# An attention and feed-forward layer whose split activation h is stored with its two parts interleaved

## What is computed

```
x = fwht(x * SU_ug) / 64
x_up   = x @ W_up.T   * (Wscale_ug[:2048] * 64)
x_gate = x @ W_gate.T * (Wscale_ug[2048:] * 64)
h = silu(x_gate) * x_up                      # 4096 tokens x 2048
x = fwht(h * SU_dp) / 64
x = x @ W_down.T * (Wscale_dp * 64)          # back to 512 columns
```

## Time and profile before

| | us |
|---|---|
| median of 3 runs | 1592.2 |
| lowest and highest run | 1590.52 and 1594.0 |
| the profiled execution's own time | 1590.71 |
| its span, from the first to the last instruction | 1588.9 |

### The profile page before, as it was taken

The page is one execution under the profiler, slowest core; times in us unless marked ns, Lnnn a source line. Parts: engine busy times, 40 slices in busy tenths (PEclk is TensorE's granted clock), DMA queues, the critical chain, the costliest instruction groups (busy, mean ns, idle before and its releaser), DMA issues.

```text
span 1588.9 us, 26579 instructions
## 1 busy us (share of the span) xinstructions
PE 1537.9 (97%) x10280; PEld 1385.6 (87%) x10280; DVE 1040.3 (65%) x1771; ACT 616.2 (39%) x1257; POOL 465.6 (29%) x584
## 2 busy tenths in 40 slices
PE   6999999999998799999999999999999999999997
PEld 5987988888887688889999999999999999999996
DVE  6766776677676699875575475566466557557544
ACT  4153244235225555433433343343343333333322
POOL 5365456447337533500030030030040021013001
PEclk9999999999999999999999999999999999999999
DMA  7031122122222497587668677857776867766861
GB/s 270 1 120 60 34 87 93 34 81 100 70 77 84 185 374 275 212 293 278 236 218 297 220 253 246 279 204 257 268 245 220 307 203 258 276 242 212 281 229 63
DMA packets 92060, 307.44 MB, mean 193 GB/s; under 512 B 9888, under 2 KB 10272, under 8 KB 90144
## 3 DMA queue, kind: packets, MB, share of 16 engines
q1 hardware_dynamic: 90928, 301.54, 53.8%
q10 hardware_dynamic: 1008, 4.20, 0.7%
HBM read 255.37 MB, written 50.33 MB: 192 GB/s over the span
## 4 chain that ended last, share of the span: by engine, by line
PE 61%; DVE 5%; ACT 1%; DMA 1%; issue 1%; SPq 0%; POOL 0%; ACTq 0%; POOLq 0%; DVEq 0%
PE ff_bank_b L1840 16%; PE ff_bank_c L1840 10%; PE ff_bank_a L1840 10%; PE ff_acc L105 7%; PE ff_acc L107 7%; PE ff_acc L106 7%; DVE ff_d_lo L1639 2%; DMA gu_scratch<-ff_ring 1%; DVE ff_ring L1629 1%; PE ff_x_ps L1791 1%; ACT at_union L578 1%; PE ff_x_ps L1811 1%; PE ff_x_ps L1799 0%; DVE ff_c L1685 0%; PE ff_x_ps L1800 0%
## 5 line engine op out<-in xcount | busy, mean ns | idle before, releaser
L1840 PE MATMUL ff_bank_b<-ff_x_hi,ff_ring 128*128 128x256 f32 x1536 | 303.5, 280 | 4.5 <-DVE ff_c L1685 4.2
L1840 PEld LDWEIGHTS ff_bank_b<-ff_x_hi,ff_ring 128*128 128x128 f32 x1536 | 248.6, 188 | 6.3 <-issue 4.5
L1840 PE MATMUL ff_bank_b<-ff_x_lo,ff_ring 128*128 128x256 f32 x768 | 214.7, 280 | 0.0
L105 PE MATMUL ff_acc<-ff_d_hi,ff_h_hi 128*128 128x512 f32 x512 | 203.9, 398 | 2.7 <-DVE ff_d_lo L1639 2.7
L1840 PE MATMUL ff_bank_c<-ff_x_hi,ff_ring 128*128 128x256 f32 x1024 | 205.8, 284 | 0.0
L1840 PE MATMUL ff_bank_a<-ff_x_hi,ff_ring 128*128 128x256 f32 x1024 | 203.5, 282 | 0.0
L107 PE MATMUL ff_acc<-ff_d_hi,ff_h_lo 128*128 128x512 f32 x512 | 199.8, 390 | 0.0
L106 PE MATMUL ff_acc<-ff_d_lo,ff_h_hi 128*128 128x512 f32 x512 | 199.4, 389 | 0.0
L1840 PEld LDWEIGHTS ff_bank_c<-ff_x_hi,ff_ring 128*128 128x128 f32 x1024 | 166.2, 189 | 2.2 <-issue 2.0
L1840 PEld LDWEIGHTS ff_bank_a<-ff_x_hi,ff_ring 128*128 128x128 f32 x1024 | 165.3, 188 | 2.7 <-DVE ff_ring L1629 0.2
L1679 DVE TENSOR_TENSOR ff_c<-ff_bank_b,ff_c 128x512 f32<-128x512 f32 x64 | 44.2, 690 | 163.8 <-PE ff_bank_b L1840 163.8
(11 more groups left out here) (306 smaller groups left out, 3523.7 us busy)
## 6 DMA issues: line engine op xcount, KB each, us to landing
ff_ring<-gu_scratch SPq DMA_DIRECT2D x392, 512.0 KB, 4.9
gu_scratch<-ff_ring SPq DMA_DIRECT2D x56, 512.0 KB, 7.6
at_xt<-in_xt SPq DMA_DIRECT2D x4, 2048.0 KB, 8.4
at_xn<-in_x SPq DMA_DIRECT2D x32, 256.0 KB, 3.0
x_scratch<-at_x SPq DMA_DIRECT2D x32, 256.0 KB, 2.0
ff_raw<-in_wgu SPq DMA_DIRECT2D x8, 1024.0 KB, 7.7
at_wd_a<-in_wd SPq DMA_DIRECT2D x8, 512.0 KB, 4.1
mixed_scratch<-at_wd_a SPq DMA_DIRECT2D x8, 512.0 KB, 3.5
```

Source lines behind the costliest of these rows:

```text
L105: pe.matmul(out, lhs_hi, rhs_hi, start=first, stop=False)
L1840: i = pe.matmul(bank[:, m, :], r[:, a, m, c, :], b[:, k, c, :], start=(k < 3 and m == 0 and c == 0 and b is x_hi and a == 0), stop=(m == 1 ...
```

## The change

The two parts of h get one tile per buffer, with an innermost axis of two; the high part is element 0 of that axis, the low part element 1. Everything that reads or writes `h_hi` and `h_lo` keeps its code and now goes through these views.

```diff
-        h_hi = [sb(f"h_hi{i}", [P, 2, FB], F32R) for i in range(2)]
-        h_lo = [sb(f"h_lo{i}", [P, 2, FB], F32R) for i in range(2)]
+        h = [sb(f"h{i}", [P, 2, FB, 2], F32R) for i in range(2)]
+        h_hi, h_lo = [h[i][:, :, :, 0] for i in range(2)], [h[i][:, :, :, 1] for i in range(2)]
```

## The result

Seven runs of each kernel: before 1592.2 us (1590.52 to 1594.49), after 1598.95 us (1597.36 to 1602.27); the ratio is 1.005 [1.004, 1.0059]. The change costs 6.75 us, 0.4%. That lies in the range of the prediction, but the forecast case, no effect that can be told, is refuted.

A forecast was written before the change was run, and what follows sets the result against it. The prediction took TensorE to bound the kernel. Its terms for weight loads, the matmul beside them, and ScalarE and VectorE were all 0, leaving the median at 1592 us; range 1588 to 1609 us.

The forecast's parts named there:

- the forecast case: Whole kernel: no effect that can be told, 1589 to 1595.4 us; chance 58%.
- What bounds the kernel: TensorE, busy for 97% of the span; one nanosecond more per down matmul is 1.5 us.
- Weight load, taken at 112 ns: The 1536 down weight loads: stepped load as long as a contiguous one, hidden under 227 ns matmuls, 0 us.
- The upper bound of 224 ns: Down weight loads: twice the contiguous time, still hidden inside a down, 4.5 us at 42 entries behind 256-column matmuls.
- doubled loads: Down entries: loads of twice the length make the first down matmul 106 ns late, 4.5 us in all; chance 7%.
- the cliff: Down matmuls: loads of 336 ns pass 227 ns and set the pace, costing 167 us; chance 6%.
- ScalarE and VectorE: Rounding and subtraction of h: stepped access adds at most 0.41 us per instruction, taken as 0 because of slack.
- The first block: VectorE, 88% busy there: sixteen longer subtractions add up to 6.6 us, 1599 us; chance 4%.
- "Does a load slow the matmul beside it? I take 0": The 1536 down matmuls: stepped load's effect on the stream beside it, taken as 0, upper end 16.3 us.
- that rival: Down matmuls' streaming operand: load reads collide with it, twice the lines touched, up to 16.3 us, 1608.5 us; chance 17%.
- The 10.6 ns: Extra time per full-rate fp32r 512-column matmul over plain fp32 (13.7 against 3 ns excess), from load reads or type.
- The faster rival: Down matmuls: new spacing parts loads and streams meeting at unlucky addresses, at most -16.3 us, half of that 1584; chance 8%.

The follow-up runs named there:

- s32: The kernel after with all parts of h in one tile, elements 32 bytes apart in the down weight loads: 1625.11 us, 1.0205.
- ring8: The kernel before with gate and up weights interleaved in the ring, so the multiplies' weight loads step 8 bytes, h plain: 1607.97 us, 1.0102.
- rd8: The kernel before, h written plain, but down weight loads read every second element (wrong elements, same work): 1598.66 us, 1.0045.
- wr8: The kernel after, h still written with the step, but down weight loads read adjacent elements (wrong elements, same work): 1592.46 us, 1.0005.
- ah8: The kernel after with h 8 KB lower, ahead of sg and hf, step of 8 bytes: 1599.45 us, 1.0047 to before.
- b0: The kernel before with each down weight load reading one element 128 times (wrong product, same work): 1595.54 us, 1.0032.
- sh16: The kernel before, no step, with h moved 16 bytes further on: 1596.07 us, 1.0034.
- sh64: The kernel before, no step, with h moved 64 bytes further on: 1598.84 us, 1.0053.
- sh208: The kernel before, no step, with h moved 208 bytes further on: 1599.61 us, 1.0052.
- sh16s: The kernel after, step of 8 bytes, with h moved 16 bytes further on: 1596.36 us, 1.0027 to before.
- s16: The kernel after with both parts and buffers of h in one tile, elements 16 bytes apart in the down weight loads: 1610.71 us, 1.0117.
- ahc: The kernel before, no step, with h 8 KB lower, ahead of sg and hf: 1592.8 us, 1.0009.
- place: The kernel before, no step, with the low part's tiles behind all others, where hi8 has them: 1589.15 us, 0.9982.
- hi8b: Repetition of hi8 on another chip with more rounds: 1591.46 us against 1592.05 for the kernel before, 0.9994.
- lo8: Only the low part of h stepped by 8 bytes, the high part's tiles plain and behind all others: 1593.22 us, 1.0011 to before.
- hi8: Only the high part of h stepped by 8 bytes, the low part's tiles plain and behind all others: 1588.31 us, 0.9977 to before.

## Why the prediction was right and wrong

- **What bounds the kernel: right.** Within some 2 us every result is the sum of what the downs and the multiplies gained or lost: s32 +33.9 us by its downs, +33.0 measured; ring8 +14.3 and +15.9; rd8 +7.2 and +6.5.
- **Weight load, taken at 112 ns: right within 6 ns** (111 and 118), and hidden. The upper bound of 224 ns was far too high, and with it went the rivals of doubled loads (1596.7 us) and of the cliff (1759 us): entries cost nothing. The picture drawn for doubled loads, a late entry and a pace hardly changed, comes at 16 bytes, where the record is 309 ns, the loads at an entry start 0.21 us apart and the pace is 235.
- **ScalarE and VectorE: right in the cost of 0.** ScalarE takes 48 ns more, VectorE 1, of the 410 allowed; wr8 shows that it costs nothing that can be told. The first block grew by 2.6 us in the profiled execution of after, but not in that of ah8, which has the same step; what lengthened the wait is open.
- **"Does a load slow the matmul beside it? I take 0": the step that failed.** It measured 6 ns between the steady paces, 4.6 on the mean, 1536 x 4.6 = 7.1 us. The threshold that the prediction gave for that rival, 2.1 ns, was passed, and its sign in the profile came: a pace of 233 in the span 229 to 238, with nothing late at the entries, though the load's record was not unchanged (194 ns for 188). The argument for 0 was "nothing ties the excess to the load"; wr8 and rd8 tie it to the load's reads.
- **But the rival was right only in part.** The load's reads do slow the stream; the lines touched don't make the price: b0, sh16, sh64 and sh208, none of which has a step, have 232 or 233 ns as well. What is shown: the kernel before has h at a place (the same 8 KB lower) where adjacent reads stream at 227 ns, the best pace of all kernels here, and the step gives that up; where it is given up already, the step costs nothing (sh16 and sh16s). The prediction said that the change "shifts no other tile" and took addresses into account for the gain alone, as "unlucky addresses". It was before that had the lucky ones. That the measured time falls inside the stated range is owed to the room that the range left for its slower rivals, not to the sum. The 10.6 ns from which this rival's price came stay unexplained. They compare with plain fp32 taken as two passes; the rows show only its 430 ns, which is twice 213.3 and 3 more, and no run took the 10.6 away.
- **The faster rival** (a part of the 10.6 ns goes) names the right thing, addresses, with the wrong sign.
- The Trainium skill, TensorE: Matmul & The Clock Gate, section Step-by-step, has it that a load takes no bandwidth from a running matmul. The runs don't show it so: with the streams and the clock the same, and loads of 111 to 118 ns that a down hides, the pace is 227 or 232 to 233 ns by what the load beside it reads and from where.

Moving h was all that these runs tried, and the tiles behind it (`y1`, the small ones) moved too; wr8, whose tiles lie as in after and whose pace is 227, shows for the original place that the reads alone decide. In the moved kernels the writes to h and the other moved tiles were not separated from the reads.

Open: by what rule load and stream disturb each other. The pattern is exactly repeatable and the same 8 KB lower; moves of 16, 64 and 208 bytes break it. Whether s16 and s32 are bound by their loads or by slowed streams, and so why 32 bytes cost more than 16 at equal lines, is not known, nor whether a place exists that keeps 227 ns with the step: only three were tried. Moving the streaming operand was not tried. The account is good to some 2 us: rd8 measures 0.7 us less than its downs say, sh208 1.9 more (+9.2 for +7.2 us). sh16 and b0 measure 2.5 and 1.9 less, but their multiplies are 0.4 and 0.3 ns faster than before's 117.6, which is 2.3 and 1.5 us.

## What to carry to other kernels

A step of 8 bytes in four-byte elements costs little in itself: a weight load +6 ns, a ScalarE write +48 on 621, a VectorE instruction +1. Behind matmuls of 256 columns, which hardly hide a load, even that showed (ring8, +1.0%). A step of 16 bytes took the load's record from 188 to 309 ns and the writes from 621 to 1154, and shows where a short matmul has to hide a load. When a layout edit moves a TensorE-bound kernel by half a per cent, time the old layout 16 and 64 bytes further on before the edit is blamed, and the new one too. In the account of such a kernel a nanosecond per matmul matters, so read the distances of starts by position, not the mean record.

## What the runs showed that was not expected

- The distance between back-to-back fp32r matmuls of 512 columns at full clock depends on the bytes' place: 227 ns at best, 232 or 233 on the mean with h moved by 16 to 208 bytes (single distances from 227 to 236), 245 with weights 32 bytes apart. It repeats from down to down and from chip to chip.
- Moving the low part of h behind the other tiles (and the high part of the second buffer by 4 KB), without a step, makes the 5376 multiplies, which read none of h, 1.3 ns faster each (117.6 to 116.3, -7 us). In sh208, 208 bytes of gap ahead of h, they stayed at 117.65. The cause stays open.
- Reading one element 128 times is no cheaper for a load (188 ns) and gives the matmul beside it 232 ns, 5 more than 128 adjacent elements at the same place.
- After an idle time of 2.66 us the clock fell to its 1.2 GHz level for six to eight matmuls: at once in after, rd8, ah8 and sh208, from the fourth to the seventh matmul on in ahc, place, hi8b and sh64. It stayed high after the same wait in before, wr8, sh16, sh16s, lo8, hi8, b0 and ring8. What decides is open. In the first block it fell after a wait of 2.00 us in after and not after 1.61 us in before.
